# Low-rank rows and listed rows turned by VectorE instead of TensorE in a two-layer low-rank expert kernel

## What is computed

```python
x = x + _L0_ffn_ref(_L0_cond_ref(x, ...), ...)   # grouped convolution over 9 taps, then
#   base_out = x @ base_w.T + base_b ; res_hidden = x @ A.T        (rank 64)
#   combine = top-2 of 16 experts ;  delta = sum_e combine_e * res_hidden @ B_e.T
x = x + _L1_ffn_ref(_L1_cond_ref(x, ...), ...)   # 64 x 64 mixing per sample, then
#   base = xf @ base_W.T ; h = xf @ lora_A.T                       (28 experts x rank 8 = 224)
#   h = h * (gate_full * SCALING)[:, :, None] ; lora_out = einsum('ner,eor->no', h, lora_B)
```

## Time and profile before

| | us |
|---|---|
| median of 3 runs | 1221.04 |
| lowest and highest run | 1219.93, 1226.84 |
| the profiled execution, its own time | 1223.9 |
| its span, first to last instruction | 1222.0 |
| TensorE busy in the span | 1180.2 |
| VectorE busy | 701.3 |
| ScalarE busy | 774.0 |

### The profile page before, as it was taken

The page is one execution under the profiler, slowest core; times in us unless marked ns, Lnnn a source line. Parts: engine busy times, 40 slices in busy tenths (PEclk is TensorE's granted clock), DMA queues, the critical chain, the costliest instruction groups (busy, mean ns, idle before and its releaser), DMA issues.

```text
span 1222.0 us, 22071 instructions
## 1 busy us (share of the span) xinstructions
PE 1180.2 (97%) x6783; PEld 1041.7 (85%) x6783; DVE 701.3 (57%) x1989; ACT 774.0 (63%) x1761; POOL 290.9 (24%) x307
## 2 busy tenths in 40 slices
PE   6799979999999999999999999999999999999998
PEld 6799979999998998988787877777788888888887
DVE  6577768677665554656855444444455465565552
ACT  4666646666568677674476776776755656656751
POOL 2011542322222222224411211211122123222200
PEclk9899989999999999999999999999999999999999
DMA  7467656775699999988689999999964554555510
GB/s 292 156 228 277 218 180 212 280 258 194 178 294 322 328 310 317 309 294 231 150 210 292 284 276 300 300 277 294 300 176 96 133 126 92 131 120 98 125 52 35
DMA packets 85197, 267.15 MB, mean 219 GB/s; under 512 B 23458, under 2 KB 27938, under 8 KB 77859
## 3 DMA queue, kind: packets, MB, share of 16 engines
q1 hardware_dynamic: 72608, 230.12, 57.8%
q0 software_dynamic: 11264, 35.66, 16.5%
q10 hardware_dynamic: 1266, 0.70, 0.2%
HBM read 154.24 MB, written 112.20 MB: 218 GB/s over the span
## 4 chain that ended last, share of the span: by engine, by line
PE 41%; DMA 8%; DVE 2%; ACT 1%; issue 1%; SPq 0%; POOL 0%; ACTq 0%; POOLq 0%; DVEq 0%
PE z L1455 12%; PE z L1456 12%; PE z L1457 12%; DMA xin<-zs_dram,gpos 3%; DMA x<-zs_dram,gpos 2%; DMA xin<-x_dram 1%; DMA x<-x_dram 1%; PE c L1455 1%; DMA ht<-hs_dram 1%; PE c L1456 1%; PE c L1457 1%; PE c L1522 1%; PE prep L1719 1%; PE c L1526 1%; PE c L1524 0%
## 5 line engine op out<-in xcount | busy, mean ns | idle before, releaser
L749 ACT ACTIVATE moved<-mid 32x256 f32<-32x256 f32 x960 | 398.8, 415 | 123.3 <-DVE mid L1024 103.3
L1455 PE MATMUL z<-w_1h,yh 128*128 128x384 f32 (+1 forms) x512 | 191.5, 374 | 2.1 <-DVE w_1l L1144 2.1
L1455 PE MATMUL z<-w_0h,yh 128*128 128x384 f32 (+1 forms) x512 | 187.1, 365 | 0.0
L1457 PE MATMUL z<-w_1l,yh 128*128 128x384 f32 (+1 forms) x512 | 187.0, 365 | 0.0
L1457 PE MATMUL z<-w_0l,yh 128*128 128x384 f32 (+1 forms) x512 | 185.8, 363 | 0.0
L1456 PE MATMUL z<-w_1h,yl 128*128 128x512 f32 (+1 forms) x504 | 184.1, 365 | 0.0
L1456 PE MATMUL z<-w_0h,yl 128*128 128x512 f32 (+1 forms) x504 | 182.8, 363 | 0.0
L664 POOL TENSOR_TENSOR carrier<-ones_col 128x1 f32<-128x1 f32 x96 | 31.6, 329 | 558.4 <-DVE den L1118 144.8
L1455 PE MATMUL z<-w_2h,yh 128*128 128x336 f32 (+1 forms) x512 | 153.2, 299 | 3.3 <-DVE yl L1032 3.0
L1457 PE MATMUL z<-w_2l,yh 128*128 128x336 f32 (+1 forms) x512 | 152.6, 298 | 0.0
L1456 PE MATMUL z<-w_2h,yl 128*128 128x252 f32 (+1 forms) x504 | 150.1, 298 | 0.0
(11 more groups left out here) (213 smaller groups left out, 2556.7 us busy)
## 6 DMA issues: line engine op xcount, KB each, us to landing
bd<-bd_dram SPq DMA_DIRECT2D x96, 512.0 KB, 8.1
zs_dram<-zt SPq DMA_DIRECT2D x96, 512.0 KB, 9.3
hs_dram<-zt SPq DMA_DIRECT2D x34, 512.0 KB, 6.9
x8raw<-in_x_dram SPq DMA_DIRECT2D x32, 516.0 KB, 5.1
xin<-in_x_dram SPq DMA_DIRECT2D x32, 512.0 KB, 5.0
x_dram<-xb SPq DMA_DIRECT2D x32, 512.0 KB, 6.0
out_dram<-xb SPq DMA_DIRECT2D x32, 512.0 KB, 3.6
bd_dram<-bd SPq DMA_DIRECT2D x8, 1024.0 KB, 6.1
```

The source lines that it names most:

```text
L749: return nc.scalar.activation(o, i_, ACT.Copy)
L1455: T.matmul(o, ah, wh, start=start, stop=False, **kw)
L1457: return T.matmul(o, ah, wl, start=False, stop=stop, **kw)
```

## The change

TensorE's two transposes per tile are gone from both places. VectorE turns instead, SBUF to SBUF, in 16 instructions: each takes a block of 32 partitions x 32 columns (and its twin, 128 columns on, so 64 elements per partition) and writes it, turned, to another group of 32 partitions. The input group changes after every fourth instruction, the output group after every one.

- `turn_ht(s)` waits on VectorE for the four loads of `ht` and makes 16 transposes into a new tile `ht_turned`. In layer 0 it stands after the addition of block z0 and ahead of `turn_rows`; in layer 1 after `turn_rows` and ahead of `h1l`. For s = 0 and s = 12, the first ones of a wave, it stands near the end of the step, directly ahead of `ht_low`.
- `turn_hx(t)` makes 16 transposes directly behind `hx`, into `hx_turned`. The 224 columns are now 128 and 96 instead of 112 and 112, so the products have 128 and 96 rows; four of the 16 transposes have 32 columns instead of 64. `lb`, the matrix for them, is laid out for that and padded.
- The semaphores `ht_ps` and `l1_hT_ps` are now raised by VectorE. `ht_high`, `ht_low`, `h1h` and `h1l` read from SBUF instead of PSUM. The two `ht` tiles are one; `hx_turned` gets one memset more.

```diff
-K1 = ER1 // 2
+K1 = (128, ER1 - 128)
@@ scalar
-                copy(hh[:, :, :].rearrange("p j r -> p (j r)"), prepp[:, 0:PER // 2 * P]).then_inc(hh_ready, 1)
+                copy(hh[:, :, :], ht_turned[:, :, :]).then_inc(hh_ready, 1)
-                copy(h1h[:, :, :], prepp[0:K1, 0:2 * P].rearrange("p (k r) -> p k r", r=P)).then_inc(a1.hT_hi, 1)
+                copy(h1h[:, :, :], hx_turned[:, :, :]).then_inc(a1.hT_hi, 1)
@@ vector
+            def turn_ht(s):
+                for v in range(PER):
+                    dve.wait_ge(ht_in[v], 16 * s + 16)
+                for i in range(P // Q):
+                    for q in range(P // Q):
+                        mm = V.transpose(ht_turned[Q * q:Q * (q + 1), :, Q * i:Q * (i + 1)],
+                                         ht[Q * i:Q * (i + 1), :, Q * q:Q * (q + 1)])
+                mm.then_inc(ht_ps, 1)
+
+            def turn_hx(t):
+                dve.wait_ge(a1.hx, 2 * t + 2)
+                for i in range(P // Q):
+                    for q in range(P // Q):
+                        k = 2 if Q * q < K1[1] else 1
+                        mm = V.transpose(hx_turned[Q * q:Q * (q + 1), 0:k, Q * i:Q * (i + 1)],
+                                         hx1[Q * i:Q * (i + 1), 0:k, Q * q:Q * (q + 1)])
+                mm.then_inc(a1.hT_ps, 1)
@@ vector, step0
                 residual(i, u, 0)
+                if turn is not None and not at(turn, 0):
+                    turn_ht(turn)
                 turn_rows(a0, t + 1)
...
                 rank0(t, u, w)
+                if at(turn, 0):
+                    turn_ht(turn)
                 if turn is not None:
                     ht_low(turn)
@@ vector, step1
                 spread1(t)
+                turn_hx(t)
                 if late:
                     x1_low(t + 1, (v + 1) % 4)
...
                     turn_rows(a1, tiles)
+                if turn is not None and not at(turn, WS):
+                    turn_ht(turn)
                 dve.wait_ge(a1.hT_hi, t + 1)
@@ tensor
-            def turn_ht(s, first=False):
-                for v in range(PER):
-                    pe.wait_ge(ht_in[v], 16 * s + 16)
-                ...
-                for j in range(PER // 2):
-                    mm = T.transpose(prepp[:, P * j:P * (j + 1)], ht[j][:, :], ident[:, :])
-                mm.then_inc(ht_ps, 1)
@@ tensor, step1
-                pe.wait_ge(a1.hx, 2 * t + 2)
-                for k in range(2):
-                    mm = T.transpose(prepp[0:K1, P * k:P * (k + 1)], hx1[:, K1 * k:K1 * (k + 1)], ident[:, :])
-                mm.then_inc(a1.hT_ps, 1)
```

More of the change, by code:

```diff
@@ L1417, in step1 @@
                     tiles_of_lists(1)
+                if at(turn, WS):
+                    turn_ht(turn)
                 if turn is not None:
@@ L1598, in rank, with step0 @@
                     .then_inc(rank_ps, 1)
-            def step0(t, u, w, first=False, tables=False, lists=False, turn=None):
+            def step0(t, u, w, first=False, tables=False, lists=False):
                 s = t - S0_LISTS
@@ L1662, in step0 @@
                     rank(t, w)
-                if turn is not None:
-                    turn_ht(turn, first=at(turn, 0))
                 if exists(t + 2):
@@ L1686, in _, with step1 @@
             step0(TILES - 1, 1, 1)
-            def step1(t, u, first=False, last=False, late=False, tables=False, lists=False, turn=None):
+            def step1(t, u, first=False, last=False, late=False, tables=False, lists=False):
                 s = t - S1_LISTS + WS
@@ L1739, in step1 @@
                     first_tiles(1)
-                if turn is not None:
-                    turn_ht(turn)
                 if first:
```

64 lines of the change are left out of this document (29 added, 35 removed).

## The result

| | us |
|---|---|
| kernel before, runs beside it, median (lowest, highest) | 1223.94 (1219.93, 1228.59) |
| changed kernel, median (lowest, highest) | 1266.23 (1259.57, 1272.12) |
| ratio, with its 95% interval | 1.0336 (1.0304 to 1.0368) |
| the changed kernel's profiled execution, its own time | 1272.12 |
| its span | 1270.4 |

The change makes the kernel slower by 3.4%, 42 us. The direction was forecast, the size was not: 1241 us with a range up to 1264.

A forecast was written before the change was run, and what follows sets the result against it. TensorE and DMA were taken as both full in the stages with lists. Terms 15.4 + 1.6 + 3.5 + 3.8 - 4.2 = + 20.1 us gave 1244.0 us profiled, 1241 us as median, range 1224 to 1264 (8 of 10).

The forecast's parts named there:

- A turn's price: On VectorE, 16 transposes starting 0.24 us apart: 3.8 us for ht, about 3.7 for hx, range 2.1 to 4.8.
- The choice between 2.1 and 3.8 us: VectorE turn: 2.1 us if transposes overlap (rival, chance 0.12, 1225 us), 3.8 us if nothing overlaps, as taken.
- Layer 0, s = 1 to 11: Layer 0 with lists: ScalarE's zt behind yh delays the convolution 1.4 us in each of eleven tiles, + 15.4 us.
- s = 0: Layer 0, first list turn: standing ahead of ht_low and conv_out, it delays the listed pair, + 1.6 us.
- the backlog would shrink by itself in layer 0: Layer 0 with lists: rows 1.3 us late at the first tile, but longer tiles let DMA catch up; nothing added.
- Layer 1, step 0: Turn of hx ahead of x1_low and z1's low weights, for which TensorE already waits: + 3.5 us.
- Layer 1 with lists: Turn of ht waits for loads, making over_h late; loss taken once, + 3.8 us, with 35 us as other end.
- loads don't catch up: Rival, chance 0.12: the lag after issue stays, layer 1 loses up to 35 us, 1255 to 1272 us.
- The clock: Rival, chance 0.10: TensorE's idle time lowers its clock in 11 layer-0 tiles, 1.7 us per fall, 19 us, 1260 us.
- The sign that was named for it: Profile slices from the 11th to the 18th with a clock under 9 tenths would show the falling clock.
- Layer 1 without lists: Steps 13 to 31: turn of hx fits VectorE's 4.44 us idle time, TensorE saves 0.22 us each, - 4.2 us.
- step 15: Layer 1: same order as step 0 but no weights behind the turn, VectorE early enough, loss 0.

The follow-up runs named there:

- e4: Changed kernel with each transpose writing to the group of 32 partitions it reads, so blocks stay in the wrong groups: 1244.94 us.
- e10: Changed kernel loading only the high half of each expert's matrix bd from the second list step of each wave on: 1246.97 us.
- e6: Changed kernel with ten thrown-away TensorE products before the wait for zt in tiles 18 to 28: 1269.3 us.
- e9: Changed kernel with two ht tiles, loads a step earlier, ht's layer-0 turn in two halves, hx's turn behind w1's low parts in steps 0 and 15: 1238.28 us.
- e12: e9 with only the high half of bd loaded from the second list step of each wave on: 1221.34 us.
- e5: Kernel before with only hx turned on VectorE, in layer-1 steps 0 and 15 behind the low parts of w1 and the counts: 1220.66 us.
- e7: Changed kernel with two ht tiles and their loads issued one list step further ahead: 1255.39 us.

## Why the prediction was wrong, step by step

**A turn's price: right.** 16 x 0.24 = 3.8 us was forecast, 16 starts 0.25 us apart and 3.97 us were measured, a single transpose lasting 235 ns. The choice between 2.1 and 3.8 us by the `mixl` pair of the earlier trace rows was the right one; e4 shows the other end.

**Layer 0, s = 1 to 11: the mechanism right, the term too small.** The chain of the prediction stands in the timeline link by link: turn, `turn_rows`, `yh`, `zt`, convolution. From the end of the addition of z0 to the convolution the prediction had 6.96 us (412.44 to 419.4); the trace has 7.21 us (425.68 to 432.89): 0.13 of the difference is the turn. Add the 0.1 that was taken off for slack, and 1.4 us per tile becomes 1.6 to 1.8. The wait's row has 21.1 us in 11 tiles, of which the longest is 3.5 us, in tile 19, where one instruction of the lists' bookkeeping (`match`, L1285) took 2.93 us ahead of the turn. Add the 2.4 us of s = 0 (next paragraph) and take off about 2 us that TensorE's own turns no longer take (18.7 against 18.9 us a tile): some 5 of the 26.6 us are left. They fit the clock: by the windows shown with e10 its mean in this stage was 0.98, so up to 4.7 us, and e6 shows that this part comes and goes. That the backlog would shrink by itself in layer 0 was right: the turn never waits there, and the DMA share is 0.92 instead of 1.01.

**s = 0: + 1.6 us forecast.** In the changed kernel TensorE stands idle for 1.78 us before the first listed pair of tile 18. The whole tile is 2.4 us longer in e9 and e12, where the other turns don't hold it up.

**Layer 1, step 0: + 3.5 us forecast, + 4.6 measured.** The idle time is 6.45 us where 5.5 was forecast. The 2.11 us from before and the turn (3.85) make 5.96 of it; the rest isn't traced. e5 gives 3.9 us of the stage back by order alone.

**Layer 1 with lists: the step that failed.** It forecast + 3.8 us, and + 22.8 were measured. The prediction said: "a TensorE that is late by 3.6 us finds the next load 3.6 us older. So the loss is taken once, at its largest". The first part holds for one step; the second is wrong. The windows of the changed kernel in step 5 of layer 1, behind the stall of step 4 (columns as above):

```profile
736.00:739.00 3.00, 3.00 (x15) 2.49 (x14) 2.79 (x12) 2.85 (x8) 0.00 (x0) 1.00 1.08 277
739.00:742.00 3.00, 3.00 (x19) 2.24 (x19) 2.84 (x11) 2.92 (x8) 1.52 (x2) 1.00 0.38 74
742.00:745.00 3.00, 3.00 (x17) 2.22 (x14) 2.45 (x6) 2.95 (x7) 0.24 (x1) 1.00 0.69 94
745.00:748.00 3.00, 3.00 (x14) 2.25 (x12) 2.84 (x13) 2.93 (x7) 0.19 (x1) 1.00 1.11 247
```

Behind a stall the DMA engines run dry, at 0.38 and 0.69. In each of the steps 5, 7, 9 and 11 there are 3 us with a share of 0.6 or less (down to 0.1); in the steps 4 to 12 of the kernel before no 3 us have under 0.87. The program gives the reason: the loads of `bd` and the stores of `zs` are issued only when TensorE and ScalarE have worked off the ones before. The time that the loads have won is not kept as a lead: the queue stands empty in it. Then all is issued at once and the backlog is back a step later. The trace shows it in the distance from the first issue of `ht` to its last landing: 13.4 to 14.1 us in the steps 4, 6, 8, 10 and 12, and 7.9 to 9.8 us in the steps between. VectorE waits 3.5 to 4.8 us in the first and not at all in the others. The prediction knew that the queue was full and took it for a reason why a late consumer finds its data. But over the stage the share before is 1.03, no room at all, and where two resources are full, each us in which either stands still is lost. The rival "loads don't catch up" (1255 to 1272 us, chance 0.12) came nearer to the measured 1266 us, for a wrong reason: the lag isn't fixed, as e10 shows.

Of the 22.8 us of this stage 17.3 are the waits before `over_h` and 1.96 a wait before z2 of step 3. The pairs that TensorE saves give back 0.34 x 11 = 3.7 us (21.83 to 21.49 in steps without a wait), and the 2.5 us that the queue cost the kernel before (its steps of 22.9 and 23.2 us) are in the waits now. This leaves 22.8 - 17.3 - 2.0 + 3.7 + 2.5 = 9.7 us, and the clock's mean of 0.96 over 265.5 us is at most 10.6 us: the sum closes with it.

**The clock: a rival that came in part.** It had a chance of 0.10 as a case of its own. It came as a companion of the longer stalls: mean 1.00 before, 0.98 and 0.96 after, in the two stages with lists. In 331 to 334 us and 369 to 372 us it was 0.70 and 0.62; the idle time just before was 1.78 and 3.52 us:

```profile
331.00:334.00 3.00, 2.05 (x10) 1.63 (x12) 1.54 (x8) 1.97 (x5) 0.00 (x0) 0.70 1.03 412
...
369.00:372.00 3.00, 2.50 (x12) 2.50 (x13) 2.66 (x11) 1.73 (x4) 0.37 (x2) 0.62 0.99 213
```

Of the eight further idle times of 1.78 to 1.81 us in layer 0 one was followed by a fall; of the five of 2.6 to 4.0 us before `over_h` in layer 1 four were. Together with the stalls it should have been a term of the sum, not an alternative to it. The sign that was named for it, slices with a clock under 9 tenths from the 11th to the 18th, was too coarse: there is none.

**Layer 1 without lists: the mechanism right, the exact sum partly luck.** - 4.2 us was forecast and measured. VectorE's idle time before `turn_rows` hides the turn. But a plain step gave 0.26 us, not 0.22, and step 15, forecast at nothing, took 0.4 us more (19.41 against 19.05); e5, which moves the turn in that step, takes 18.81.

**What stays open.** Not shown is why in e7 and in e9 the gathered rows of just this stretch come 6 to 8 us late, while the kernel before, with the same bytes, has no such stall: both have the DMA engines full, and both lose it in step 10. And which part of the whole time the clock's falls make up can't be said for the medians, only for the profiled executions.

## What to carry to other kernels

Before work is moved to an idle engine, look for the longest single gap in that engine's order, not at its busy share: 4 us in one piece cost about 20 us in 11 tiles, the same 4 us in two halves in gaps of 2.2 and 2.4 us cost nothing in nine of e12's. A wait that moves with the work is to be costed by what stands behind it; and where DMA is full over the whole stage, a stall isn't made good in the next step, since a stalled kernel doesn't issue the next transfers. If both a wait and a fall of the clock are possible, they belong in one sum.

## What the runs showed of the hardware

- 32-partition transposes of 64 elements start 0.13 us apart on one group of partitions (e4) and 0.25 us apart when the output group changes each time (changed kernel), the duration of one being 0.19 to 0.24 us. A 128 x 128 block turned so, across groups, takes VectorE 3.97 us for two blocks; TensorE's two instructions cost 0.26 us of its time (18.17 against 17.91 us per step without lists).
- Some VectorE instructions last until an addition of GpSimd is over. All 21 VectorE instructions of the kernel before and all 19 of the changed one that last over 0.4 us longer than usual start while (or at most 0.04 us before) GpSimd's addition `xb<-xin,bias0b` (2.4 us) runs, and end 0.1 to 0.2 us sooner than that addition's end plus their usual time: `match` 2.93 us instead of 0.69, `x8_low` 3.45 instead of 1.19 (e9), 3.33 in tile 27 of the kernel before. The transposes and the additions that read a block z met the same addition without being longer. No run moved GpSimd's addition, so this is read from the traces and not tested.
- A DMA share of about 1.0 is compatible with a stage that loses nothing (before: 242.7 us) and with one in which every engine stands still for 3 us (e9, 835 to 838 us). The share alone doesn't tell whether the transfer that is awaited lands in time.
